# Token dispatch on one core: fp32 contraction replaced by three products of high and low parts, phi streamed per block, slot outputs kept in the slots' buffer

## The chip, the cores and the metric

The kernel runs on 1 core of one Trainium2 chip. The metric is the device time in microseconds (us) of one execution. TensorE (PE) multiplies matrices, VectorE (DVE), ScalarE (ACT) and GpSimd (POOL) work on elements, SyncE (SP) issues most DMAs. Each engine takes its instructions in order and waits on semaphores where the code says so.

## The reference

Two transformer layers with layer norms behind each half. The first three halves (dilated attention, a switch of 8 experts, linear attention) are hardly touched by the change. The last half is a soft mixture over 64 experts with 32 slots each:

```python
logits = jnp.einsum('bmd,dnp->bmnp', x, phi)
dispatch = jax.nn.softmax(logits, axis=0)
combine = jax.nn.softmax(logits.reshape(bsz, m, n * p), axis=-1).reshape(bsz, m, n, p)
slots = jnp.einsum('bmd,bmnp->bnpd', x, dispatch)
y = jnp.einsum('bnpd,nde->bnpe', slots, W) + b[None, :, None, :]
out = jnp.einsum('bnpd,bmnp->bmd', y, combine)
```

Here b is 4, m is 1024, d is 256, n*p is 2048. The dispatch softmax is taken over the 4 batch entries, so its sum (the "share" of each entry) is local to a token and a slot.

## The kernel before, in words

The program is a chain of stages, each a block in which every engine has its own instruction list: attention, routing, the 8 experts, linear attention (`linear_attention`), then `dispatch` and `combine`. Between stages all engines meet.

`dispatch` cuts the 2048 slots into 8 blocks of 256 columns (k) and the tokens into 8 chunks of 128 per batch entry (mc). A step (k, mc) handles all 4 batch entries. Blocks 1 to 7 are a hardware loop. In a step:

- TensorE computes the logits (`score`, L1621): 4 entries x 2 halves of d x 3 products of high and low parts (x high by phi high, x high by phi low, x low by phi high) in type fp32r, 24 matmuls of 256 columns. All of phi and its parts lie in SBUF; linear attention loads and splits them.
- ScalarE copies the logits from PSUM in two halves (L1688), and takes the exponential (L1706) behind VectorE's subtraction.
- VectorE takes the maximum over the 4 entries in three operations, each with one input in PSUM (L1778, L1780, L1782), subtracts it in two (L1786, L1788), inverts the sum of the step before (L1770), and reduces the rows to a maximum for the combine stage (L1793).
- GpSimd adds the four exponentials (L1730, L1732) and multiplies those of the step before by the inverse (`share`, L1723).
- TensorE contracts x with the shares three steps later (LAG is 3, `contract`, L1636): 8 matmuls in plain fp32, which run as 16 instructions.

Twice in a block, in steps 4 and 5, TensorE also runs an expert block (L1649): half of the y of the block before, 8 fp32 matmuls (16 instructions) into PSUM bank 1. VectorE adds the bias on the way to SBUF (`copy_y`, L1760, at the start of steps 5 and 6), and SyncE stores y. SyncE's list in a block is: the logits' store of each step (`keep`, L1575), behind those of steps 5 and 6 the four stores of one y half (L1568), and at the end the weights and the bias of all 8 experts of the block (L1562, L1563). The bias is there long before it is used.

Where PSUM is shared, a step's score waits for `less`, the count of VectorE's subtractions: in steps 5 and 6 for that of the step right before, in step 7 for both y halves to have left bank 1. In step 2 of a block ScalarE and VectorE each copy one half of the finished slots to SBUF.

## Time and profile before

| what | value |
|---|---|
| median of 3 runs | 1495.3 us (1493.47 to 1497.02) |
| the profiled execution | 1496.07 us, its span 1494.3 us |
| TensorE busy over the span | 92% |
| VectorE, ScalarE, GpSimd busy | 59%, 41%, 46% |
| granted TensorE clock, mean | 0.962 of 2.4 GHz |
| dispatch, then combine | 751 to 1245 us, 1245 us to the end |

The span runs from the first to the last instruction. A row of the timeline gives start and length in us, the engine, the line, the operation, output and inputs, and in brackets how long the engine was idle before and what released it. An engine's next instruction can start a little before the end of the one before is recorded, so what an instruction occupies is read from start to start.

### The profile page before, as it was taken

How to read it: one execution, taken by the hardware profiler on the slowest of the kernel's cores; microseconds unless marked ns; L12 is line 12 of the kernel's file. 1: busy time of each engine (PE TensorE's matmuls, PEld its weight loads, DVE VectorE, ACT ScalarE, POOL GpSimd, SP SyncE). 2: the span in 40 equal slices, each digit the busy share in tenths (PEclk: the TensorE clock that was granted, in tenths of full speed). 3: DMA queues.
4: the chain of work that ended last, by engine and by line, in shares of the span. 5: the costliest groups of instructions: out<-in, count | busy, mean ns of one | idle time of the engine just before them, and what ended most of it. 6: DMA issues, size and time to landing. Idle time of an engine off the chain costs nothing. (4 is left out here: it accounts for less than half of the span.)

```text
span 1494.3 us, 27884 instructions
## 1 busy us (share of the span) xinstructions
PE 1378.0 (92%) x8959; PEld 1203.4 (81%) x8960; DVE 877.4 (59%) x1763; ACT 612.8 (41%) x1077; POOL 683.3 (46%) x556
## 2 busy tenths in 40 slices
PE   7996599899999993899879999999999997999997
PEld 3454488788888883777669999999999977999997
DVE  5788422222222223577578787887887853666655
ACT  4554323233333331766543332332333324555553
POOL 6663287777660004340026665665655644350500
PEclk9998699999999996999979999999999998999999
DMA  4102325222310004310032264464463577465450
GB/s 166 60 28 94 119 81 149 95 98 101 124 70 14 14 15 134 120 57 1 1 127 85 85 183 123 142 170 110 146 193 96 157 222 270 154 214 184 147 201 31
DMA packets 109194, 171.17 MB, mean 115 GB/s; under 512 B 6128, under 2 KB 95088, under 8 KB 101712
## 3 DMA queue, kind: packets, MB, share of 16 engines
q1 hardware_dynamic: 100112, 156.00, 32.2%
q0 software_dynamic: 3408, 9.31, 2.2%
q10 hardware_dynamic: 5616, 5.11, 1.0%
q8 instruction: 33, 0.54, 0.2%
q14 instruction: 25, 0.20, 0.0%
HBM read 114.96 MB, written 55.44 MB: 114 GB/s over the span
## 5 line engine op out<-in xcount | busy, mean ns | idle before, releaser
L1636 PE MATMUL disp_psS<-disp_e,last_x 128*128 128x256 f32 x1024 | 233.1, 381 | 4.0 <-POOL disp_e L1723 4.0
L1636 PEld LDWEIGHTS disp_psS<-disp_e,last_x 128*128 128x128 f32 x1024 | 191.2, 191 | 28.6 <-POOL disp_e L1723 4.6
L1621 PE MATMUL disp_psL<-phi_hold,hand_xh 128*128 (+1 forms) x1024 | 199.8, 296 | 4.6 <-DVE disp_e L1788 4.4
L1730 POOL TENSOR_TENSOR disp_s<-disp_e 128x512 f32<-128x512 f32 x64 | 82.3, 1286 | 264.4 <-ACT disp_e L1706 264.4
L1909 PE MATMUL comb_psO<-phi_hold,comb_eh 128*128 (+1 forms) x1024 | 197.6, 290 | 0.4 <-DVE comb_el L2007 0.3
L1621 PEld LDWEIGHTS disp_psL<-phi_hold,hand_xh 128*128 128x128 f32 x1024 | 165.1, 193 | 8.5 <-issue 5.5
L1688 ACT ACTIVATE disp_raw<-disp_psL 128x512 f32<-128x512 f32 x128 | 76.4, 597 | 222.3 <-PE disp_psL L1621 157.8
L1909 PEld LDWEIGHTS comb_psO<-phi_hold,comb_eh 128*128 128x128 f32 x1024 | 156.3, 189 | 1.0 <-DVE comb_el L2007 0.9
L1723 POOL TENSOR_TENSOR disp_e<-disp_e,disp_rs 128x1024 f32<-128x1024 f32 x64 | 151.5, 2368 | 0.0
L1621 PE MATMUL disp_psL<-phi_hold 128*128 (+1 forms) x512 | 145.7, 285 | 0.0
L1909 PE MATMUL comb_psO<-phi_hold,comb_el 128*128 (+1 forms) x512 | 143.7, 281 | 0.0
L2007 DVE TENSOR_TENSOR comb_el<-comb_psT,comb_eh 128x512 fp32r<-128x512 f32 x128 | 88.1, 689 | 90.6 <-ACT comb_eh L1943 88.0
L972 PE MATMUL moe_psH<-w_hi,moe_xh 128*128 x312 | 129.1, 414 | 6.9 <-POOL w_lo L882 5.0
L1064 DVE TENSOR_TENSOR moe_hs<-moe_psH,moe_act_a 128x1024 f32<-128x1024 f32 x39 | 47.8, 1225 | 149.0 <-PE moe_psH L972 149.0
L972 PE MATMUL moe_psH<-w_lo,moe_xh 128*128 x312 | 125.6, 403 | 0.0
L972 PE MATMUL moe_psH<-w_hi,moe_xl 128*128 x312 | 125.6, 403 | 0.0
L1072 DVE TENSOR_TENSOR moe_hl<-moe_psHT,moe_hh 128x1024 fp32r<-128x1024 f32 x39 | 47.8, 1225 | 129.9 <-ACT moe_hh L1042 129.9
L1943 ACT ACTIVATE comb_eh<-comb_psT 128x512 fp32r<-128x512 f32 x128 | 76.3, 596 | 108.6 <-PE comb_psT L1895 108.5
L1770 DVE RECIPROCAL disp_rs<-disp_rs 128x256 f32<-128x256 f32 x64 | 111.5, 1743 | 0.5 <-POOL disp_rs L1732 0.5
L1166 POOL DMA_INDIRECT lin_yg<-sorted_y,table_place x32 | 32.1, 1002 | 172.3 <-POOLq L890 139.0
L1621 PEld LDWEIGHTS disp_psL<-phi_hold 128*128 128x128 f32 x512 | 98.8, 193 | 0.0
L1909 PEld LDWEIGHTS comb_psO<-phi_hold,comb_el 128*128 128x128 f32 x512 | 96.3, 188 | 0.0
(259 smaller groups left out, 3112.1 us busy)
## 6 DMA issues: line engine op xcount, KB each, us to landing
logits<-disp_raw SPq DMA_DIRECT2D x64, 512.0 KB, 4.1
hand_e<-logits SPq DMA_DIRECT2D x32, 1024.0 KB, 6.6
w_raw<-in_w SPq DMA_DIRECT2D x8, 2048.0 KB, 7.9
disp_wt<-in_w_slot SPq DMA_DIRECT2D x16, 1024.0 KB, 7.9
w_raw<-in_w SPq DMA_DIRECT2D x8, 1024.0 KB, 10.4
disp_bt<-in_b_slot SPq DMA_DIRECT2D x8, 1024.0 KB, 11.3
slot_y<-disp_yb SPq DMA_DIRECT2D x60, 128.0 KB, 3.2
comb_y_in<-slot_y SPq DMA_DIRECT2D x3, 2048.0 KB, 10.5
```

The lines of the kernel that those rows point to most:

```text
L972: last = nc.tensor.matmul(psH[:, n, :], xpart[:, k, :], wpart[:, bass.ds(b, 1), cols].rearrange("p a f -> p (a f)"), start=first, stop=k = ...
L1064: v.tensor_tensor(hs[:], psH[:, 2:4, :].rearrange("p a b -> p (a b)"), act_a[:], ALU.mult).then_inc(hs_ready, 1)
L1072: v.tensor_tensor(hl[:], psHT[:], hh[:].bitcast(F32), ALU.subtract).then_inc(hl_ready, 1)
L1621: last = nc.tensor.matmul(psL[p][:, b, :], xp[:, kd, t * P:(t + 1) * P], pp[:, kd, bass.ds(k * BLK, BLK)], start=b % 2 == 0 and kd == 0 an ...
L1636: last = nc.tensor.matmul(psS[kd][:, b, :], x[:, b * TB + mc, kd * P:(kd + 1) * P], e[mc % 4][:, b, :], start=mc == 0 and b % 2 == 0, stop ...
L1688: nc.scalar.activation(raw[mc % 4][:, half * 2:half * 2 + 2, :], psL[l_bank[mc]][:, half * 2:half * 2 + 2, :], ACT.Copy).then_inc(copied, 1)
L1723: nc.gpsimd.tensor_tensor(e[mc % 4][:], e[mc % 4][:], rs[mc % 2][:].unsqueeze(1).to_broadcast([P, B, BLK]), ALU.mult).then_inc(share_ready, 1)
L1730: nc.gpsimd.tensor_tensor(s2[:], e[mc % 4][:, 0:2, :], e[mc % 4][:, 2:4, :], ALU.add).then_inc(pair_sum, 1)
L1770: v.reciprocal(rs[mc % 2][:], rs[mc % 2][:]).then_inc(rsum_ready, 1)
L1909: last = nc.tensor.matmul(psO[j % 2][:, 0:D], ep[s % EB][:, i, :], yp[:, bass.ds(odd, 1), ch * D:(ch + 1) * D].rearrange("p a d -> p (a d) ...
L1943: nc.scalar.activation(eh[s % EB][:], psT[s % EB][:], ACT.Copy).then_inc(hi_ready, 1)
L2007: v.tensor_tensor(el[s % EB][:], psT[s % EB][:], eh[s % EB][:].bitcast(F32), ALU.subtract).then_inc(lo_ready, 1)
```

## The change: what it does

1. `contract` uses three fp32r products (x high by share high, x high by share low, x low by share high), 24 matmuls of 256 columns in place of 8 in fp32. The high part of the shares is a copy by ScalarE (`high_of_share`, 128x1024) two steps after the exponential (EH_LAG). The low part is a subtraction in place, entries 0 and 1 by VectorE (`first_rest`, 128x512, before the inversion), entries 2 and 3 by GpSimd (`second_rest`, 128x512, behind `share`).
2. The high part of x by rows (`natural`) is made by GpSimd in linear attention for 24 of 32 row tiles and by ScalarE in dispatch for 8; the low part by GpSimd at the start of dispatch, in 16 operations of 128x512 ahead of its first step, in the place of x.
3. The maximum over the entries takes two operations in place of three: one of 128x512 from PSUM into `pair`, one of 128x256 that reads both inputs from SBUF.
4. phi is loaded in blocks of 256 columns and split in dispatch (ScalarE and VectorE, 128x512 each, in step 4 of the block before). Linear attention no longer loads or splits it.
5. y is written over the half of the slots that its expert block has read, and stored from there. The bias has a buffer for 4 experts only: that of the second half is loaded behind the stores of the first.
6. Slots leave PSUM in two operations for each half of d, all four on ScalarE in the loop.
7. `combine` adds the low and the high part of x to the output, one more 128x256 operation of VectorE for each of 32 tiles. Some semaphores are merged, and the scratch for GpSimd's descriptors is 8192 bytes.

The core of the diff:

```diff
+            def load_bias(first):
+                sp.dma_start(bt[:], b_dram[bass.ds(first, HALF), :].partition_broadcast(P)).then_inc(b_loaded, 16)
...
-                        store(k - 1, last[y_step[mc - 1]], y_step[mc - 1], yb)
+                        h = y_step[mc - 1]
+                        store(k - 1, last[h], h)
+                        load_bias(last[1] if h == 0 else here)
...
-                wait(pe, share_ready, g + 1)
-                if isinstance(k, int) and k == 0 and mc == 0:
-                    wait(pe, lo, PIECES)
+                wait(pe, first_low, g + 1)
...
-                        last = nc.tensor.matmul(psS[kd][:, b, :], x[:, b * TB + mc, kd * P:(kd + 1) * P], e[mc % 4][:, b, :],
-                                                start=mc == 0 and b % 2 == 0, stop=mc == MC - 1, skip_group_check=True)
+                        if kd == 0 and b == 2:
+                            wait(pe, second_low, g + 1)
+                        row, cols = b * TB + mc, slice(kd * P, (kd + 1) * P)
+                        for a, (xp, ep) in enumerate(((natural, eh[mc % 2]), (natural, el[mc % 4]), (natural_lo, eh[mc % 2]))):
+                            last = nc.tensor.matmul(psS[kd][:, b, :], xp[:, row, cols], ep[:, b, :],
+                                                    start=mc == 0 and b % 2 == 0 and a == 0, stop=mc == MC - 1 and a == 2,
+                                                    skip_group_check=True)
                 last.then_inc(gone, 1)
...
+            def high_of_share(g, mc):
+                wait(act, share_ready, g + 1)
+                wait(act, gone, g - 1)
+                nc.scalar.activation(eh[mc % 2][:], e[mc % 4], ACT.Copy).then_inc(eh_ready, 1)
...
+                wait(act, kept[mc % 4], k * (MC // 4 * 16) + mc // 4 * 16)
+                wait(act, peaked, g - 3)
+                copy_half(g, mc, 1)
+                wait(act, top_ready, 2 * g + 1)
+                copy_half(g, mc, 0)
+                if mc >= EH_LAG or not fresh:
+                    high_of_share(g - EH_LAG, (mc - EH_LAG) % MC)
+                if mc == SPLIT_AT:
+                    high_of_phi(k + 1, after)
                 if mc == EVAC and not fresh:
                     wait(act, gone, k * MC)
...
+                    evacuate(0)
+                wait(act, less, 2 * g + 2)
+                nc.scalar.activation(e[mc % 4], e[mc % 4], ACT.Exp).then_inc(exp_ready, 1)
+                if mc == EVAC and not fresh:
+                    evacuate(1)
...
+            def natural_rest(n):
+                wait(pool, turned, n + 1)
+                wait(pool, hi, highs(n) + n % 2)
+                nc.gpsimd.tensor_tensor(rows_of(natural_lo, n), rows_of(x, n), rows_of(natural, n).bitcast(F32),
+                                        ALU.subtract).then_inc(natural_low, 1)
+
+            def second_rest(g, mc):
+                wait(pool, eh_ready, g + 1)
+                nc.gpsimd.tensor_tensor(el[mc % 4][:, 2:4, :], e[mc % 4][:, 2:4, :], eh[mc % 2][:, 2:4, :].bitcast(F32),
+                                        ALU.subtract).then_inc(second_low, 1)
...
-
+                    second_rest(g - 1, (mc - 1) % MC)
+
+            for n in range(PIECES):
+                natural_rest(n)
...
+            def first_rest(g, mc):
+                wait(dve, eh_ready, g + 1)
+                v.tensor_tensor(el[mc % 4][:, 0:2, :], e[mc % 4][:, 0:2, :], eh[mc % 2][:, 0:2, :].bitcast(F32),
+                                ALU.subtract).then_inc(first_low, 1)
...
+            def copy_y(k, h, bank=Y_BANK):
                 wait(dve, y_raw, k * 2 + (h + 1))
-                wait(dve, b_loaded, k * 16 + 16)
-                wait(dve, stored, k * (2 * 16 * B) + h * (16 * B))
-                v.tensor_tensor(yb[:], psL[Y_BANK][:], bt[:, h * HALF:(h + 1) * HALF, :],
-                                ALU.add).then_inc(y_ready, 1)
+                wait(dve, b_loaded, k * 32 + (h + 1) * 16)
...
-                v.tensor_tensor(t[:], psl[:, 0, :], raw[mc % 4][:, 2, :], ALU.max).then_inc(top_ready, 1)
-                wait(dve, top_ready, 3 * g + 1)
-                v.tensor_tensor(t[:], psl[:, 1, :], t[:], ALU.max).then_inc(top_ready, 1)
-                wait(dve, top_ready, 3 * g + 2)
-                v.tensor_tensor(t[:], psl[:, 3, :], t[:], ALU.max).then_inc(top_ready, 1)
+                v.tensor_tensor(pair[:], psl[:, 0:2, :], raw[mc % 4][:, 2:4, :], ALU.max).then_inc(top_ready, 1)
+                wait(dve, top_ready, 2 * g + 1)
+                v.tensor_tensor(t[:], pair[:, 0, :], pair[:, 1, :], ALU.max).then_inc(top_ready, 1)
                 wait(dve, gone, g - 3)
-                wait(dve, top_ready, 3 * g + 3)
+                wait(dve, top_ready, 2 * g + 2)
                 both = t[:].unsqueeze(1).to_broadcast([P, 2, BLK])
                 v.tensor_tensor(e[mc % 4][:, 2:4, :], psl[:, 2:4, :], both, ALU.subtract).then_inc(less, 1)
                 wait(dve, copied, 2 * g + 2)
                 v.tensor_tensor(e[mc % 4][:, 0:2, :], psl[:, 0:2, :], both, ALU.subtract).then_inc(less, 1)
+                if mc >= EH_LAG or not fresh:
+                    first_rest(g - EH_LAG, (mc - EH_LAG) % MC)
                 if mc > 0 or not fresh:
                     invert(g - 1, (mc - 1) % MC)
-                if mc == EVAC and not fresh:
-                    copy_slots(k)
+                if mc == SPLIT_AT:
+                    low_of_phi(k + 1, after)
                 v.tensor_reduce(rowmax[:].rearrange("p (b j) k -> p b j k", b=B)[:, :, mc, bass.ds(k, 1)].rearrange("p b a -> p (b a)"),
                                 raw[mc % 4][:], X, ALU.max).then_inc(peaked, 1)
 
             for mc in range(MC):
-                step(0, mc, fresh=True)
...
-                v.scalar_tensor_tensor(xo[:, j, :], psO[j % 2][:, 0:D], rden[:, j % 2:j % 2 + 1], row(t), ALU.mult, ALU.add).then_inc(summed, 1)
-                wait(dve, summed, t + 1)
+                v.scalar_tensor_tensor(xo[:, j, :], psO[j % 2][:, 0:D], rden[:, j % 2:j % 2 + 1],
+                                       natural_lo[:, bass.ds(t, 1), :].rearrange("p a d -> p (a d)").bitcast(F32), ALU.mult, ALU.add).then_inc(summed, 1)
+                wait(dve, summed, 2 * t + 1)
+                v.tensor_tensor(xo[:, j, :], xo[:, j, :], natural[:, bass.ds(t, 1), :].rearrange("p a d -> p (a d)").bitcast(F32),
+                                ALU.add).then_inc(summed, 1)
+                wait(dve, summed, 2 * t + 2)
```

Three places where the order of instructions moves. First GpSimd, the looped part of dispatch, two steps of before (`disp_s` is the pairwise sum, `disp_rs` the sum and its inverse, `disp_e` the exponentials and shares):

```order
L1730 TENSOR_TENSOR disp_s<-disp_e 128x512 [waits disp_sum_ready,disp_exp_ready]
L1732 TENSOR_TENSOR disp_rs<-disp_s 128x256 [waits disp_pair_sum]
L1723 TENSOR_TENSOR disp_e<-disp_e,disp_rs 128x1024 [waits disp_rsum_ready]
L34 REGISTER_ALU
L1730 TENSOR_TENSOR disp_s<-disp_e 128x512 [waits disp_sum_ready,disp_exp_ready]
L1732 TENSOR_TENSOR disp_rs<-disp_s 128x256 [waits disp_pair_sum]
L1723 TENSOR_TENSOR disp_e<-disp_e,disp_rs 128x1024 [waits disp_rsum_ready]
```

The same place now (`disp_eh`, `disp_el` are the high and low parts of the shares; 7965 to 7968 are the four buffers of `disp_e`):

```order
L1803 TENSOR_TENSOR disp_s<-disp_e_7965 128x512 [waits disp_sum_ready,disp_exp_ready]
L1805 TENSOR_TENSOR disp_rs<-disp_s 128x256 [waits disp_pair_sum]
L1796 TENSOR_TENSOR disp_e_7968<-disp_e_7968,disp_rs 128x1024 [waits disp_rsum_ready]
L1791 TENSOR_TENSOR disp_el<-disp_e_7968,disp_eh 128x512 [waits disp_eh_ready]
L34 REGISTER_ALU
L1803 TENSOR_TENSOR disp_s<-disp_e_7966 128x512 [waits disp_sum_ready,disp_exp_ready]
L1805 TENSOR_TENSOR disp_rs<-disp_s 128x256 [waits disp_pair_sum]
L1796 TENSOR_TENSOR disp_e_7965<-disp_e_7965,disp_rs 128x1024 [waits disp_rsum_ready]
L1791 TENSOR_TENSOR disp_el<-disp_e_7965,disp_eh 128x512 [waits disp_eh_ready]
```

Each step has gained L1791, which waits for ScalarE's high part, ahead of the next step's sum. Second, ScalarE in one step of the loop now (before, the two copies of the logits L1688 and the exponential L1706 alone):

```order
L1735 ACTIVATE disp_raw<-disp_psL 128x512 [waits disp_peaked,disp_kept2,disp_logits]
L34 ISA
L1735 ACTIVATE disp_raw<-disp_psL 128x512 [waits disp_top_ready]
L1728 ACTIVATE disp_eh<-disp_e_7965 128x1024 [waits disp_gone,disp_share_ready]
L34 REGISTER_ALU
L1760 ACTIVATE disp_e_7967<-disp_e_7967 128x1024 [waits disp_less]
```

The high part of a share (L1728) stands ahead of the exponential of two steps later (L1760). Third, VectorE around the second y copy of the loop, now:

```order
L1868 TENSOR_TENSOR disp_top<-disp_pair 128x256 [waits disp_top_ready]
L34 REGISTER_ALU [waits disp_gone]
L1872 TENSOR_TENSOR disp_e_7966<-disp_psL,disp_top 128x512 [waits disp_top_ready]
L1874 TENSOR_TENSOR disp_e_7966<-disp_psL,disp_top 128x512 [waits disp_copied]
L1836 TENSOR_TENSOR disp_el<-disp_e_7968,disp_eh 128x512 [waits disp_eh_ready]
L1858 RECIPROCAL disp_rs<-disp_rs 128x256 [waits disp_sum_ready]
L1881 ISA
L1881 TENSOR_REDUCE last_rowmax<-disp_raw 128x4
L34 REGISTER_ALU
L34 REGISTER_ALU [waits disp_y_raw]
L1846 TENSOR_TENSOR disp_slots<-disp_psL,disp_bt 128x1024 [waits disp_b_loaded]
L34 ISA
```

L1868 and L1836 read both inputs from SBUF and are new. The y copy, L1846, waits for the bias, and all of step 6 on VectorE is queued behind it.

## Rows read from the trace of the kernel before

**Rows 1.** Busy time in one stretch of the dispatch, by engine (columns as named).

```profile
880.00:930.00 50.00, 50.00 (x308) 46.38 (x308) 39.66 (x50) 16.31 (x22) 29.29 (x22) 1.00 0.42 115
```

**Rows 2.** Timeline of TensorE: start, length, idle before in brackets.

```profile
862.78 0.28 PE L1621 MATMUL disp_psL<-phi_hold 128*128 x1
...
863.14 0.28 PE L1621 MATMUL disp_psL<-phi_hold 128*128 x1
...
865.42 3.62 PE L1636 MATMUL disp_psS<-disp_e,last_x 128*128 128x256 f32 x16
868.69 0.59 PE L1621 MATMUL disp_psL<-phi_hold,hand_xh 128*128 x2
```

**Rows 3.** Timeline of the same step: VectorE, ScalarE and GpSimd.

```profile
866.25 0.42 DVE L1778 TENSOR_TENSOR disp_top<-disp_psL,disp_raw 128x256 f32<-128x256 f32 x1 [0.93 <-ACT disp_raw L1688]
866.71 0.42 DVE L1780 TENSOR_TENSOR disp_top<-disp_psL,disp_top 128x256 f32<-128x256 f32 x1
...
867.62 0.69 DVE L1786 TENSOR_TENSOR disp_e<-disp_psL,disp_top 128x512 f32<-128x512 f32 x1
...
868.83 1.74 DVE L1770 RECIPROCAL disp_rs<-disp_rs 128x256 f32<-128x256 f32 x1
868.95 1.06 ACT L1706 ACTIVATE disp_e<-disp_e 128x1024 f32<-128x1024 f32 x1 [1.19 <-DVE disp_e L1788]
...
870.08 1.29 POOL L1730 TENSOR_TENSOR disp_s<-disp_e 128x512 f32<-128x512 f32 x1 [1.92 <-ACT disp_e L1706]
...
870.49 1.16 DVE L1793 TENSOR_REDUCE last_rowmax<-disp_raw 128x1024 f32 x1
...
871.46 0.73 POOL L1732 TENSOR_TENSOR disp_rs<-disp_s 128x256 f32<-128x256 f32 x1
...
872.14 2.36 POOL L1723 TENSOR_TENSOR disp_e<-disp_e,disp_rs 128x1024 f32<-128x1024 f32 x1
```

**Rows 4.** Timeline of the two steps with an expert block, third block of slots.

```profile
900.54 3.62 PE L1649 MATMUL disp_psL<-disp_wt,disp_slots 128*128 128x256 f32 x16
...
908.62 0.60 ACT L1688 ACTIVATE disp_raw<-disp_psL 128x512 f32<-128x512 f32 x1 [0.95 <-DVE disp_top L1780]
...
910.05 2.48 SPq L1568 DMA_DIRECT2D slot_y<-disp_yb  x4
...
914.55 1.22 DVE L1760 TENSOR_TENSOR disp_yb<-disp_psL,disp_bt 128x1024 f32<-128x1024 f32 x1 [1.45 <-DMA slot_y<-disp_yb]
...
917.49 0.42 DVE L1778 TENSOR_TENSOR disp_top<-disp_psL,disp_raw 128x256 f32<-128x256 f32 x1 [1.71 <-ACT disp_raw L1688]
```

**Rows 5.** Groups by line: count, then least, median and largest ns.

```profile
L1498 POOL TENSOR_TENSOR phi_hold<-hand_y,phi_hold x4: 1258/2336/2356, 1236.0 to 1242.9; 128x1024 fp32r<-128x1024 f32 x3, 128x512 fp32r<-128x512 f32 x1
L1498 DVE TENSOR_TENSOR phi_hold<-hand_y,phi_hold x1: 684/684/684, 1251.7 to 1251.7; 128x512 fp32r<-128x512 f32 x1
...
L1491 ACT ACTIVATE phi_hold<-hand_y x5: 612/1038/1056, 1234.8 to 1250.9; 128x1024 fp32r<-128x1024 f32 x3, 128x512 fp32r<-128x512 f32 x2
```

**Rows 6.** Timeline of the last stage: VectorE and GpSimd side by side.

```profile
1281.58 0.73 POOL L1884 TENSOR_TENSOR phi_hold<-comb_y_in,phi_hold 128x256 fp32r<-128x256 f32 x1
...
1281.76 0.57 DVE L47 TENSOR_TENSOR comb_mean<-comb_stats 128x4 f32<-128x4 f32 x1
...
1282.26 0.15 DVE L48 TENSOR_TENSOR comb_var<-comb_stats 128x4 f32<-128x4 f32 x1
```

**Rows 7.** Timeline, start of the dispatch: its first contraction.

```profile
780.09 1.13 PE L1636 MATMUL disp_psS<-disp_e,last_x 128*128 128x256 f32 x4 [1.97 <-POOL disp_e L1723]
```

**Rows 8.** Timeline of TensorE: last looped expert block, and the final pair.

```profile
1188.41 1.89 PE L1649 MATMUL disp_psL<-disp_wt,disp_slots 128*128 128x256 f32 x8
...
1228.64 7.14 PE L1649 MATMUL disp_psL<-disp_wt,disp_slots 128*128 128x256 f32 x32 [1.52 <-DVE disp_slots L1765]
```

**Rows 9.** DMA issues of the page: count, KB each, median us to landing.

```profile
logits<-disp_raw SPq DMA_DIRECT2D x64, 512.0 KB, 4.1
...
disp_bt<-in_b_slot SPq DMA_DIRECT2D x8, 1024.0 KB, 11.3
```

More of the change, by code:

```diff
@@ L1180, in _ @@
                     fetch(t)
[L1181 to L1182 removed]
+            pool.wait_ge(constants_set, KB + 2)
+            for t in range((B - 1) * TB):
+                natural_high(t)
         @block.tensor
@@ new lines, in step @@
+            def step(k, mc, after, fresh=False):
+                g = k * MC + mc
+                wait(act, logits, g + 1)
+                wait(act, kept[mc % 4], k * (MC // 4 * 16) + mc // 4 * 16)
[7 more added lines that the diff above has]
+                    high_of_phi(k + 1, after)
@@ L1711, in _ @@
                 for mc in range(MC):
-                    step(k, mc)
-            step(NBLK, EVAC, draining=True)
+                    step(k, mc, bass.ds(other, 1))
+            for mc in range(MC - EH_LAG, MC):
+                high_of_share((NBLK - 1) * MC + mc, mc)
+            wait(act, gone, NBLK * MC)
+            evacuate(0)
             act.wait_ge(hand.neg_ready, 2)
```

244 lines of the change are left out of this document (138 added, 106 removed).

## The prediction, made before the changed kernel ran

> **What bounds the kernel now.** I read the busy shares first, then a stretch inside the dispatch, then a step of it engine by engine. In the stretch TensorE is busy 50.00 of 50.00 us at full clock, VectorE 39.7, GpSimd 29.3, ScalarE 16.3 [rows 1]. So today nothing but TensorE's own work sets the dispatch, and a cheaper contraction would be gained in full, as long as the other three stay hidden. Two numbers for that. A triple of fp32r products takes 863.14 - 862.78 = 0.36 us, 0.12 per matmul; a contraction takes 868.69 - 865.42 = 3.27, and the fp32r matmul behind it starts about 0.18 late (the first row's length is 0.59, not about 0.40), so 3.45 in all [rows 2]. A step is then 24 x 0.12 + 3.45 = 6.33.
>
> The other engines, start to start [rows 3]: on GpSimd pair sum to sum 1.38, sum to share 0.68, share 2.36, so 4.42 from the first to the end. On VectorE a 256-column maximum 0.46, the two subtractions 1.21 (one 0.61, its length 0.69), the inversion 1.66, the row maximum about 1.09. On ScalarE the exponential 1.06. GpSimd was idle 1.92 before its pair sum and VectorE 0.93 before its maximum: this is the whole cover, a step.
>
> A block of 8 steps and two expert blocks takes (1188.41 - 900.54) / 5 = 57.57 us [rows 4, 8]. In its sixth step the second y copy waits 1.45 for the store of the first half, and still VectorE is idle 1.71 before its next maximum: harmless today [rows 4].
>
> **The change, part by part.**
>
> TensorE: a contraction falls from 3.45 to 24 x 0.12 = 2.88. That is 0.57 a step; 64 of them are 36 us. That gain exists only if a step of the others fits in 5.76.
>
> The loop through GpSimd and ScalarE. The new low part on GpSimd waits for ScalarE's high part, which waits for the share, and the next pair sum stands behind it. So a step cannot be shorter than: pair sum to share end 4.42 [rows 3], high part of 1024 columns 1.04, low part of 512 columns on GpSimd 1.26 [rows 5], three hand-overs of about 0.04 to 0.08 (exponential end 870.01, pair sum 870.08): **6.85 us**. This loop did not exist before. It is above 5.76 and also above 6.33.
>
> The second SBUF input. VectorE's new 256-column maximum and its low part read two operands from SBUF; the old ones had one in PSUM. The trace of the last stage shows what such an operation does beside GpSimd: an operation on 4 columns starts at 1281.76, takes 0.57 and ends at 1282.33, just behind the GpSimd operation that ends at 1282.31, and the next one like it takes 0.15 [rows 6]. So it waits until the running GpSimd operation is over. In the new step the maximum comes when the share is under way: VectorE's low part ends, inversion 1.66, row maximum 1.09, the 512-column maximum with its hand-over 0.73, together 3.48 after the pair sum started, while the share runs from 2.06 to 4.42. The chain of a step becomes: share end 4.42, maximum 0.46, first subtraction 0.61, second 0.69, exponential 1.06, hand-overs 0.15: 7.39. Then VectorE's low part, held until GpSimd's own low part ends (4.42 + 0.04 + 1.04 + 0.08 + 1.26 = 6.84), has read for 0.66 more, to **7.5 us** a step, which I take. The bounds are 6.85 (no such wait) and 7.5.
>
> The Trainium skill states this as a rule ("SBUF — State Buffer", Who interferes with whom): a VectorE instruction with two SBUF inputs contends with a GpSimd instruction that reads SBUF, and whichever starts first holds the shared port for its whole length. The trace agrees. By the rule a step is 7.5, without it 6.85.
>
> The bias. The load for the second half is issued only behind the four stores of the first half. The logits' copy of step 5 ends, and 0.83 later the first store is issued (909.22 to 910.05), which take 2.48 [rows 4]; then the load. Its landing is bounded by a store of the same 512 KB, 4.1, and half of the 1024 KB bias load, 5.65 [rows 9]. Counted from the pair sum of step 3 in a block (0): share, maximum and exponential of step 4 put its sum at 7.5; phi's low part, held behind the sum, and the row maximum bring VectorE to 11.25; first y copy to 12.4 (1.15 [rows 4]); logits' copy of step 5 over at 13.7; stores to 17.05; load issued at 17.25, landed at 21.35 to 22.9. TensorE's second expert block is done at about 15.9 and step 6's logits could be used at 19.85, so VectorE now stands still for the bias, and the maximum of step 6 comes at 22.55 to 24.1. The pair sum of step 6 follows 4.3 later (0.73 + 0.60 + 1.04 + 0.66 + 1.26), at 26.9 to 28.4. Five more steps of 7.5 and 0.3 for ScalarE's copy of the slots ahead of an exponential: a block is 64.7 to 66.2, middle 65.4, **+7.8** over 57.57. Queued behind the y copy is all of VectorE's step 6, and TensorE's step 7, which needs bank 1, waits too. Had the load landed in time, step 6's sum would be at 24.15 and a block at 62.0.
>
> Start of the dispatch. It begins at about 751 with a load of phi, 3 us by my estimate (under the 4.1 of 512 KB [rows 9]), ahead of ScalarE's first high part, then GpSimd does its 16 subtractions, 16 x 1.22 = 19.5, from about 755.2 to 774.7. Two sums, a share, high and low part add 4.1 + 2.4 + 1.1 + 0.7, to 783.0, and the exponential of step 1, itself about 2 later, to at most 785; I take 784.8 in place of 780.09 [rows 7]. Nine steps of 7.5, 0.3 for the slots, 0.6 for phi's low part and 2.9 for a contraction bring the first expert block to 856.1, where it was 900.54 - 57.57 = 842.97: **+13.1**. Six blocks of 7.8: **+46.8**.
>
> The end. From the last looped expert block to the final pair was 1228.64 - 1188.41 = 40.2 [rows 8]. Now 27.65 to the pair sum of step 6, 7.5 to that of step 7, then two shares with their high and low parts and the last contraction, 14.6, and 1.7 to the expert block as before, less the 3.0 by which it starts behind the sum: 48.45, **+8.2**. The last y half waits for a bias load too: four stores and 4.1 to 5.65 of landing against no wait, less a quicker last store: 1 to 5, I take **+3**. Combine: one more operation of VectorE a tile, of which the last shows, **+0.5**.
>
> At nothing: linear attention loses two copies of phi on ScalarE and 16 subtractions on GpSimd and gains 24 operations there, beside a TensorE that they did not hold up; the merged semaphores keep their order; the smaller scratch could hold GpSimd's gathers back by up to a landing of 4.1 [rows 9]; they come ahead of stages that no row shows short of them, and I take 0.
>
> Sum: 13.1 + 46.8 + 8.2 + 3 + 0.5 = 71.6 on the profiled execution's 1496.07, 0.8 above the median of the runs, so about **1566**.
>
> **The rivals.**
>
> No wait for the second SBUF input. The 0.57 was seen on tiny operations; if large ones interleave, a step is 6.85. Then the first expert block comes 7.3 later, a block takes 60.3 (+2.7, six of them 16.4), the end costs 4.9 + 3 + 0.5: +32, about 1528. With the bias in time too, a block is 57.4 and the total about 1507. Rows 6 speak against it.
>
> TensorE stays the bound, the other side. If GpSimd's and ScalarE's loop were shorter than 5.76 (it decides at 5.76; my sum says 6.85), a block would be 57.57 - 8 x 0.57 = 53.0, less 36 in all, plus 4.7 at the start and 3 at the end: 1467. For it: 50.00 of 50.00 us busy, and spacings of new pairs of operations that no row shows. Against it: 1.1 us a step would have to vanish from instructions whose lengths are in the rows.
>
> A lower TensorE clock. TensorE would now idle 7.5 - 5.76 = 1.7 a step, and longer at the bias. The clock was lower behind the gap at the start: contraction instructions there start 1.13 / 4 = 0.28 apart, not 0.20 [rows 2, 7]. At half clock a step of TensorE is 11.5; six such steps among 64 add 24: about 1590.
>
> **How the numbers follow.** The forecast, loop, second input and bias together, 0.57; no wait for the second input 0.16, and with the bias in time 0.04; TensorE the bound 0.11; the clock case or worse 0.12. The first two hold 0.73. The range from 1520 to 1588 takes in the step between 6.85 and 7.5, the bias between 4.1 and 5.65, and part of the clock case, some 0.8. A change of under 0.2% (3 us) could not be told from none; faster 0.12, same 0.03, slower 0.85.
>
> **What would show it.** In the looped part: pair sums on GpSimd 7.5 us apart (6.85 in the first rival, 5.8 in the second), ended by ScalarE; the 256-column maximum recorded at well over 0.46, ending with the share; VectorE's second y copy waiting some 3 to 4 us for the bias; blocks of 65 us; TensorE busy about 80% of the dispatch; gaps of TensorE put down to the low parts of VectorE or GpSimd. I am wrong if TensorE is still without gaps there. The weakest step is the maximum that meets the share: a VectorE that comes 1.4 us earlier or later in the cycle misses it.

## The result, and the profile after the change

| kernel | median | runs |
|---|---|---|
| before | 1494.38 us | 1492.98 to 1497.02, 4 runs |
| changed | 1562.43 us | 1560.84 to 1562.88, 4 runs |

The ratio is 1.0447, 95% interval 1.0434 to 1.0460: the change makes the kernel 68 us slower. The forecast was 1566, range 1520 to 1588.

From the page of the changed kernel: span and busy times.

```profile
span 1559.1 us, 29192 instructions
...
PE 1363.3 (87%) x9471; PEld 1201.8 (77%) x9472; DVE 1011.9 (65%) x1799; ACT 683.7 (44%) x1178; POOL 807.4 (52%) x644
```

TensorE's share falls from 92% to 87%, VectorE's rises from 59% to 65% and GpSimd's from 46% to 52%. Busy times of the stretch that [rows 1] showed (PE, PEld, DVE, ACT, POOL; then granted clock, DMA share, GB/s):

```profile
880.00:930.00 50.00, 42.07 (x329) 40.44 (x330) 49.52 (x49) 24.16 (x32) 38.20 (x28) 1.00 0.51 142
```

TensorE, 50.00 of 50.00 before, is down to 42.07 (84%; about 80 was forecast). VectorE has gone from 39.66 to 49.52: in this stretch it has no gap left. One step of the loop, VectorE, then GpSimd, then ScalarE, against [rows 3]:

```profile
956.17 1.16 DVE L1881 TENSOR_REDUCE last_rowmax<-disp_raw 128x1024 f32 x1
957.25 0.67 DVE L1866 TENSOR_TENSOR disp_pair<-disp_psL,disp_raw 128x512 f32<-128x512 f32 x1
957.95 1.24 DVE L1868 TENSOR_TENSOR disp_top<-disp_pair 128x256 f32<-128x256 f32 x1
959.23 0.69 DVE L1872 TENSOR_TENSOR disp_e<-disp_psL,disp_top 128x512 f32<-128x512 f32 x1
959.84 0.68 DVE L1874 TENSOR_TENSOR disp_e<-disp_psL,disp_top 128x512 f32<-128x512 f32 x1
960.43 1.48 DVE L1836 TENSOR_TENSOR disp_el<-disp_e,disp_eh 128x512 fp32r<-128x512 f32 x1
961.83 1.74 DVE L1858 RECIPROCAL disp_rs<-disp_rs 128x256 f32<-128x256 f32 x1
...
956.50 2.41 POOL L1796 TENSOR_TENSOR disp_e<-disp_e,disp_rs 128x1024 f32<-128x1024 f32 x1
960.08 1.28 POOL L1791 TENSOR_TENSOR disp_el<-disp_e,disp_eh 128x512 fp32r<-128x512 f32 x1 [1.17 <-ACT disp_eh L1728]
961.68 1.37 POOL L1803 TENSOR_TENSOR disp_s<-disp_e 128x512 f32<-128x512 f32 x1 [0.32 <-ACT disp_e L1760]
963.13 0.74 POOL L1805 TENSOR_TENSOR disp_rs<-disp_s 128x256 f32<-128x256 f32 x1
...
958.94 1.06 ACT L1728 ACTIVATE disp_eh<-disp_e 128x1024 fp32r<-128x1024 f32 x1 [0.40 <-POOL disp_e L1796]
960.55 1.06 ACT L1760 ACTIVATE disp_e<-disp_e 128x1024 f32<-128x1024 f32 x1 [0.54 <-DVE disp_e L1874]
```

Read it as a circle. GpSimd's share (L1796) starts at 956.50 and ends at 958.91. VectorE's 256-column maximum (L1868), which reads both inputs from SBUF, starts at 957.95 and takes 1.24, where the shortest of its 64 in this trace takes 0.42: it ends at 959.19, 0.28 behind the share. Then subtractions, exponential (960.55), and the pair sum (L1803) at 961.68, which waited for ScalarE. It started at 954.36 the step before: 7.32. VectorE's low part (L1836) starts 0.35 behind GpSimd's own (L1791) and takes 1.48, ending 0.55 behind it. Who waited for whom between 780 and 1300 us (total us, times, longest):

```profile
PE disp_psS L1668 <- DVE disp_el L1836: 66.4, 46, 4.3
...
DVE disp_slots L1846 <- DMA disp_bt<-in_b_slot: 18.3, 7, 3.0
```

TensorE, which had no gap in the stretch of [rows 1], now waits 66.4 us for VectorE's low part. Its contraction did get cheap, 0.11 to 0.12 us from one fp32r product to the next once it runs:

```profile
961.97 0.38 PE L1668 MATMUL disp_psS<-disp_eh,last_natural 128*128 128x256 f32 x1 [1.37 <-DVE disp_el L1836]
962.19 0.28 PE L1668 MATMUL disp_psS<-disp_el,last_natural 128*128 128x256 f32 x1
```

The second half's bias, third block of slots: the y copies on VectorE, and SyncE's four stores and load.

```profile
931.48 1.21 DVE L1846 TENSOR_TENSOR disp_slots<-disp_psL,disp_bt 128x1024 f32<-128x1024 f32 x1
...
941.96 1.23 DVE L1846 TENSOR_TENSOR disp_slots<-disp_psL,disp_bt 128x1024 f32<-128x1024 f32 x1 [2.46 <-DMA disp_bt<-in_b_slot]
...
934.75 2.46 SPq L1579 DMA_DIRECT2D slot_y<-disp_slots  x4
937.41 0.38 SPq L1574 DMA_DIRECT2D disp_bt<-in_b_slot  x1
```

The load is issued at 937.41, behind the stores, and the copy waits 2.46 us for it. Expert blocks: the first of the third block, the last looped one, and the final pair.

```profile
923.59 3.62 PE L1682 MATMUL disp_psL<-disp_wt,disp_slots 128*128 128x256 f32 x16
...
1241.37 3.62 PE L1682 MATMUL disp_psL<-disp_wt,disp_slots 128*128 128x256 f32 x16
...
1290.58 7.14 PE L1682 MATMUL disp_psL<-disp_wt,disp_slots 128*128 128x256 f32 x32 [1.65 <-DVE disp_slots L1852]
```

A block takes (1241.37 - 923.59) / 5 = 63.56 us; it was 57.57 [rows 4, 8].

### The profile page after: what moved, and what is told of

The parts are those of the page before. It is cut to its first block and busy times, and to the rows that moved or that the text cites. A ratio compares the mean times of both kernels' runs of the same rounds, so it can differ in the third digit from the quotient of the medians.

```text
span 1559.1 us, 29192 instructions
## 1 busy us (share of the span) xinstructions
PE 1363.3 (87%) x9471; PEld 1201.8 (77%) x9472; DVE 1011.9 (65%) x1799; ACT 683.7 (44%) x1178; POOL 807.4 (52%) x644
## 5 line engine op out<-in xcount | busy, mean ns | idle before, releaser
L1668 PE MATMUL disp_psS<-disp_eh,last_natural 128*128 128x256 f32 x512 | 151.0, 295 | 66.8 <-DVE disp_el L1836 66.4
L2000 PE MATMUL comb_psO<-hand_parts,comb_eh 128*128 (+1 forms) x1024 | 198.6, 292 | 1.7 <-DVE comb_el L2102 1.7
L1649 PE MATMUL disp_psL<-disp_ph,hand_xh 128*128 (+1 forms) x512 | 150.4, 294 | 18.1 <-DVE disp_slots L1846 9.3
L2000 PEld LDWEIGHTS comb_psO<-hand_parts,comb_eh 128*128 128x128 f32 x1024 | 156.9, 190 | 2.8 <-issue 1.8
L1668 PEld LDWEIGHTS disp_psS<-disp_eh,last_natural 128*128 128x128 f32 x512 | 98.8, 193 | 76.7 <-DVE disp_el L1836 76.4
L1796 POOL TENSOR_TENSOR disp_e<-disp_e,disp_rs 128x1024 f32<-128x1024 f32 x64 | 157.2, 2456 | 0.0
L1649 PE MATMUL disp_psL<-disp_pl,hand_xh 128*128 (+1 forms) x512 | 146.7, 287 | 0.0
L1649 PE MATMUL disp_psL<-disp_ph,hand_xl 128*128 (+1 forms) x512 | 146.4, 286 | 0.0
L1668 PE MATMUL disp_psS<-disp_el,last_natural 128*128 128x256 f32 x512 | 145.6, 284 | 0.0
L1668 PE MATMUL disp_psS<-disp_eh,last_natural_lo 128*128 128x256 f32 x512 | 145.4, 284 | 0.0
L2000 PE MATMUL comb_psO<-hand_parts,comb_el 128*128 (+1 forms) x512 | 144.0, 281 | 0.0
L1791 POOL TENSOR_TENSOR disp_el<-disp_e,disp_eh 128x512 fp32r<-128x512 f32 x64 | 82.7, 1292 | 106.2 <-ACT disp_eh L1728 106.2
L1649 PEld LDWEIGHTS disp_psL<-disp_ph,hand_xh 128*128 128x128 f32 x512 | 100.1, 195 | 20.2 <-issue 19.9
```

The costliest lines, as they stand in the source:

```text
L1649: last = nc.tensor.matmul(psL[p][:, b, :], xp[:, kd, t * P:(t + 1) * P], pp[:, half, kd, :].rearrange("p a n -> p (a n)"), start=b % 2 == ...
L1668: last = nc.tensor.matmul(psS[kd][:, b, :], xp[:, row, cols], ep[:, b, :], start=mc == 0 and b % 2 == 0 and a == 0, stop=mc == MC - 1 and ...
L1791: nc.gpsimd.tensor_tensor(el[mc % 4][:, 2:4, :], e[mc % 4][:, 2:4, :], eh[mc % 2][:, 2:4, :].bitcast(F32), ALU.subtract).then_inc(second_l ...
L1796: nc.gpsimd.tensor_tensor(e[mc % 4], e[mc % 4], rs[mc % 2][:].unsqueeze(1).to_broadcast([P, B, BLK]), ALU.mult).then_inc(share_ready, 1)
L2000: last = nc.tensor.matmul(psO[j % 2][:, 0:D], ep[s % EB][:, i, :], yp[:, bass.ds(odd, 1), ch * D:(ch + 1) * D].rearrange("p a d -> p (a d) ...
```

## Experiments

All were compared with the kernel before on their own chip, so their ratios can be set against 1.0447. Blocks are the distance between two expert blocks.

**Is TensorE still the bound?** One fp32 product of the high parts in place of three; the low parts are computed and waited for, but left out of the product.

```diff
-for a, (xp, ep) in enumerate(((natural, eh[mc % 2]), (natural, el[mc % 4]), (natural_lo, eh[mc % 2]))):
-    last = nc.tensor.matmul(psS[kd][:, b, :], xp[:, row, cols], ep[:, b, :], ...
+last = nc.tensor.matmul(psS[kd][:, b, :], natural[:, row, cols].bitcast(F32), eh[mc % 2][:, b, :].bitcast(F32), ...
```

> The contraction is one plain fp32 product of the high parts (8 matmuls, 3.45 us as before the change) in place of three fp32r products (2.88); the low parts of shares and x are still computed and waited for, but left out of the product. My theory: TensorE is no longer the bound in the dispatch, its step of 6.33 is hidden under 7.32, so the time stays within 3 us of 1562.4, perhaps 1 to 2 more from the first and last contractions; pair sums still 7.3 apart. Rival: TensorE's own work still counts in full, +0.57 x 64 = +36, 1599.

Measured: 1559.83, ratio 1.0415 (1.0391 to 1.0440); +36 would be 1.069. Busy times of the stretch from 880 to 930 us:

```profile
880.00:930.00 50.00, 45.75 (x280) 41.63 (x279) 49.52 (x49) 24.27 (x32) 38.33 (x28) 1.00 0.50 142
```

TensorE is busy 3.7 us more and the time does not rise. Plain steps are even 0.05 shorter (7.27 for 7.32); why is not shown. The change's gain of 0.57 a step is worth nothing here, and its loss comes from the other engines.

**The two meetings, one at a time.** First without VectorE's low part (entries 0 and 1 in two products), the maximum as changed:

```diff
-                if mc >= EH_LAG or not fresh:
-                    first_rest(g - EH_LAG, (mc - EH_LAG) % MC)
```

> The changed kernel without VectorE's low part of the shares (entries 0 and 1 are contracted in two products, their low part is left out); the maximum still reads both inputs from SBUF. My theory, after the first runs: there are two meetings of VectorE and GpSimd, and each alone makes a loop: the maximum held until the share is over (7.3), and the low parts, where whichever engine starts first holds the other (7.4). Here the first is left: pair sums 7.2 to 7.3 apart, maximum 1.2 and longer, VectorE with gaps; 64 x 0.1 less, 1550 to 1562. Rival: the step was 7.32 because VectorE's list was full; 1.40 taken from it lets the loop through the high part set the step, 6.85, 1532.

Measured: 1547.79, ratio 1.0347 (1.0321 to 1.0374), a gain of 15; plain steps of 7.2.

```profile
954.13 2.55 DVE L1870 TENSOR_TENSOR disp_top<-disp_pair 128x256 f32<-128x256 f32 x1
...
954.00 2.40 POOL L1798 TENSOR_TENSOR disp_e<-disp_e,disp_rs 128x1024 f32<-128x1024 f32 x1
```

The maximum is now 2.55 us long. VectorE, with 1.4 us less to do, reaches it earlier and is only held longer, until the share is over. The rival (a full VectorE sets the step) would have given 6.85 and falls. The total is 2 us below the range forecast: the step that splits phi went from 8.54 to 7.64, which I had not counted, while the wait for the bias grew to 3.8 to 4.5 us a block (2.3 to 3.0 in the changed kernel).

Then the maximum as before, from PSUM, and VectorE's low part kept:

```diff
-v.tensor_tensor(pair[:], psl[:, 0:2, :], raw[mc % 4][:, 2:4, :], ALU.max).then_inc(top_ready, 1)
-wait(dve, top_ready, 2 * g + 1)
-v.tensor_tensor(t[:], pair[:, 0, :], pair[:, 1, :], ALU.max).then_inc(top_ready, 1)
+v.tensor_tensor(t[:], psl[:, 0, :], raw[mc % 4][:, 2, :], ALU.max).then_inc(top_ready, 1)
+wait(dve, top_ready, 3 * g + 1)
+v.tensor_tensor(t[:], psl[:, 1, :], t[:], ALU.max).then_inc(top_ready, 1)
+wait(dve, top_ready, 3 * g + 2)
+v.tensor_tensor(t[:], psl[:, 3, :], t[:], ALU.max).then_inc(top_ready, 1)
```

> The maximum over the entries is put back to three 128x256 operations with one input in PSUM; all else as in the changed kernel. My theory: the maximum that is held until the share is over sits in the loop that sets the step (pair sum to share start 2.15, share 2.41, held maximum 0.32, subtractions 1.31, exponential 1.13: 7.32). Without it the loop through the high part and GpSimd's low part is left, 6.85: pair sums 6.8 to 7.0 apart, no VectorE maximum over 0.5, VectorE with gaps again, 64 x 0.47 = 30 less, 1532 us. Rival: VectorE is simply full (it has no gap in the changed kernel) and the operations take what they take; three of 0.46 are 0.22 more than 0.70 and 0.46, so a step grows and the time goes to 1576. Second rival: the hold moves on to the low part, step 7.1, 1548.

Measured: 1558.04, ratio 1.0405 (1.0387 to 1.0422), a gain of 4 by the medians and 6 by the ratios, where I expected 30.

```profile
961.59 0.69 DVE L1836 TENSOR_TENSOR disp_el<-disp_e,disp_eh 128x512 fp32r<-128x512 f32 x1 [1.41 <-ACT disp_eh L1728]
...
955.99 1.28 POOL L1803 TENSOR_TENSOR disp_s<-disp_e 128x512 f32<-128x512 f32 x1
...
961.63 1.79 POOL L1791 TENSOR_TENSOR disp_el<-disp_e,disp_eh 128x512 fp32r<-128x512 f32 x1 [1.17 <-ACT disp_eh L1728]
963.38 1.28 POOL L1803 TENSOR_TENSOR disp_s<-disp_e 128x512 f32<-128x512 f32 x1
```

My first theory falls here in part. The maximum is 0.42 again, but VectorE is now early, and its low part (961.59) starts 0.04 before GpSimd's (961.63). Now GpSimd is held: 1.79 in place of 1.28. The pair sum behind it comes 7.39 after the last one: the loop of 6.85 and the hold of about 0.5. My second rival had this mechanism, with 7.1 for its size. The Trainium skill says so ("SBUF — State Buffer", Who interferes with whom): the order of issue decides who blocks. The traces agree, with 1.48 for VectorE behind GpSimd above, and 1.79 for GpSimd behind VectorE here.

Then both taken away, by the two edits together:

> Both meetings taken away: maximum in three operations with an input in PSUM, and VectorE's low part left out (entries 0 and 1 in two products). My theory: the loop pair sum, sum, share, high part, GpSimd's low part is left: 1.35 + 0.69 + 2.38 + 1.13 + 1.30 = 6.85, pair sums 6.8 to 6.9 apart, ended by GpSimd's own low part; 64 x 0.47 = 30 less than the changed kernel, 1532. The wait for the bias is as before or up to 1 longer a block. Rival: GpSimd's operations are slowed by VectorE's reads in general, also with one SBUF input; then the step stays over 7.1 and the time over 1548.

Measured: 1523.88, ratio 1.0189 (1.0165 to 1.0213), 39 less than the changed kernel.

```profile
951.16 1.28 POOL L1793 TENSOR_TENSOR disp_el<-disp_e,disp_eh 128x512 fp32r<-128x512 f32 x1 [1.17 <-ACT disp_eh L1730]
952.40 1.29 POOL L1805 TENSOR_TENSOR disp_s<-disp_e 128x512 f32<-128x512 f32 x1
953.77 0.74 POOL L1807 TENSOR_TENSOR disp_rs<-disp_s 128x256 f32<-128x256 f32 x1
954.47 2.40 POOL L1798 TENSOR_TENSOR disp_e<-disp_e,disp_rs 128x1024 f32<-128x1024 f32 x1
958.04 1.27 POOL L1793 TENSOR_TENSOR disp_el<-disp_e,disp_eh 128x512 fp32r<-128x512 f32 x1 [1.17 <-ACT disp_eh L1730]
```

Pair sum to pair sum in plain steps is 6.85 to 6.88: high part, low part, pair sum, sum and share in a row, the loop of the forecast. Blocks fall from 63.6 to 59.2, more than eight steps of 0.47, since the step that splits phi falls from 8.5 to 7.1. Of the 40.3 us between the two spans 26.3 are in the six blocks and 7.0 at the start, where the first expert block came 98.8 us after the dispatch's first transpose, not 105.8. The wait for the bias grew to 4.1 to 4.3 us a block, by more than the 1 I had allowed.

**The new maximum alone, in the kernel before.**

> The kernel before, with only the maximum of the change (one 128x512 operation from PSUM, one 128x256 that reads both inputs from SBUF). My theory: the new maximum is held behind the share here too, recorded at 1.2 to 1.5 us against 0.42, but TensorE is the bound at 6.33 a step, and GpSimd, which waited 1.92 before each pair sum, still waits about 1.1: no change, 1495 +- 3. Rival: the hold reaches TensorE through the logits' banks in the steps with an expert block, +1 a step there, +16 in all.

Measured: 1517.09, ratio 1.0141 (1.0124 to 1.0158): 21 us slower, although nothing of TensorE's 6.33 a step had changed. The loss is under 2%, but its interval is clear of 1.

```profile
948.17 2.49 DVE L1781 TENSOR_TENSOR disp_top<-disp_pair 128x256 f32<-128x256 f32 x1
950.69 0.69 DVE L1785 TENSOR_TENSOR disp_e<-disp_psL,disp_top 128x512 f32<-128x512 f32 x1
...
948.01 2.37 POOL L1724 TENSOR_TENSOR disp_e<-disp_e,disp_rs 128x1024 f32<-128x1024 f32 x1
953.14 1.27 POOL L1731 TENSOR_TENSOR disp_s<-disp_e 128x512 f32<-128x512 f32 x1 [2.77 <-ACT disp_e L1707]
...
960.34 1.26 POOL L1731 TENSOR_TENSOR disp_s<-disp_e 128x512 f32<-128x512 f32 x1 [2.78 <-ACT disp_e L1707]
```

My theory was wrong. The maximum, 0.42 alone, takes 2.49, and the pair sums stand 7.20 apart. The idle times of 0.93 and 1.92 [rows 3] were no cover, since each step's delay is the next step's starting point: the share ends, 0.28 later the maximum, subtractions to the exponential at 1.63, pair sum 1.13 later, share 2.04 behind that, and it runs 2.38. That circle is 7.18, longer than 6.33, and seven of a block's eight steps take it (the eighth, with the expert blocks in it, 8.9): 59.2 a block against 57.57.

**The bias.** SyncE issues the load ahead of the stores:

```diff
-                        store(k - 1, last[h], h)
+                        wait(sp, y_ready, (k - 1) * 2 + (h + 1))
                         load_bias(last[1] if h == 0 else here)
+                        store(k - 1, last[h], h)
```

> SyncE issues the load of the next half's bias ahead of the four stores of y, not behind them; nothing else differs. My theory: the second y copy of a block waits 2.46 us for a load that is issued 2.66 later than it could be, and all of VectorE's sixth step is queued behind it; seven waits of 2.46 go and part of the last one of 6.05 (1.8): 1562.4 - 17.2 - 1.8 = 1543.5, blocks of 61.2. Rival: the wait is covered, since TensorE's second expert block and the loop through GpSimd would be late anyway; then the wait is put down to another releaser and the time falls by less than 8. Second rival: the load lands later when it competes with the logits' store, a wait of 1 stays, 1553.

Measured: 1550.48, ratio 1.0362 (1.0345 to 1.0379), 13 less where 19 were expected.

```profile
937.59 1.20 DVE L1847 TENSOR_TENSOR disp_slots<-disp_psL,disp_bt 128x1024 f32<-128x1024 f32 x1
...
1061.93 1.22 DVE L1847 TENSOR_TENSOR disp_slots<-disp_psL,disp_bt 128x1024 f32<-128x1024 f32 x1 [2.07 <-DMA disp_bt<-in_b_slot]
...
932.94 0.37 SPq L1574 DMA_DIRECT2D disp_bt<-in_b_slot  x1
```

In the third block (first row) the wait is gone, and the block takes 61.2, as forecast; in the fifth (second row) it is 2.07, and each later block has one of 1.6 to 2.3. But the stores now run beside the load, whose median landing rises from 4.6 to 5.7 us, and 5 of the 16 copies still wait, 12.2 us together, against 8 and 24.3: the second rival, in part. The mean block is 62.1.

**Other orders.** Maximum from PSUM and bias first, and: the exponential ahead of the high part, GpSimd's low part behind the next pair sum, VectorE's behind the row maximum.

> Nothing left out. Maximum from PSUM, bias load first, and three orders changed so that no engine waits for the high part: ScalarE takes the exponential ahead of the high part, GpSimd's low part of two steps before stands between pair sum and sum, VectorE's low part behind the row maximum. My theory: the loop of 6.85 is gone, GpSimd's own work is 5.7 and TensorE's 5.76; the way from a score over copies, maximum, exponential, pair sum and low part to the contraction (6.9 and 5.76 for two steps) gives 6.4; VectorE's low part meets a busy GpSimd and adds up to 0.6: step 6.4 to 6.9, 1500 to 1530, most likely 1510. Rival: GpSimd has no gap any more, VectorE's low part is held behind the share of 2.4 in each step and the loop closes through it: step over 7.2, 1540 or more.

Measured: 1549.13, ratio 1.0353 (1.0328 to 1.0378). Plain steps are 6.8 to 6.9 (one of a block 6.2) as expected, but the step that copies the slots takes 8.4 and the two with an expert block 10.2 and 9.1 to 10.9. The total is the rival's, its step of over 7.2 is not. Beside the edits named, four of its blocks still wait for the bias, up to 2.9 us.

```profile
958.21 1.60 DVE L1839 TENSOR_TENSOR disp_el<-disp_e,disp_eh 128x512 fp32r<-128x512 f32 x1
...
957.97 1.28 POOL L1792 TENSOR_TENSOR disp_el<-disp_e,disp_eh 128x512 fp32r<-128x512 f32 x1
959.21 1.19 POOL L1808 TENSOR_TENSOR disp_rs<-disp_s 128x256 f32<-128x256 f32 x1
```

VectorE's low part is held behind GpSimd's to 1.60, then GpSimd's sum behind it to 1.19 (0.73 alone). The hold is passed on, not hidden. What the long steps cost each is not separated.

The whole low part on VectorE, the orders left alone (maximum from PSUM and bias first here too):

```diff
-v.tensor_tensor(el[mc % 4][:, 0:2, :], e[mc % 4][:, 0:2, :], eh[mc % 2][:, 0:2, :].bitcast(F32), ...
+v.tensor_tensor(el[mc % 4][:], e[mc % 4][:], eh[mc % 2][:].bitcast(F32), ...
-                    second_rest(g - 1, (mc - 1) % MC)
```

> Nothing left out, all 8 entries' products as in the changed kernel. Maximum from PSUM, bias load first, and the whole low part (128x1024) made by VectorE, none by GpSimd; orders as in the changed kernel. My theory: the loop then runs share end, high part 1.08, exponential 1.0, pair sum, sum, share: 4.45 + 0.04 + 1.04 + 1.0 + 0.05 = 6.6, VectorE's own list is 6.55, its low part of 1.2 falls into the time in which GpSimd waits for the exponential, so nobody is held: step 6.6 to 6.8, 1500 to 1512. Rival: the low part starts late enough to meet the pair sum, one holds the other for up to 1.2 as in the run with the maximum from PSUM alone; step 7.2 or more, 1535 and up.

Measured: 1517.67, ratio 1.0154 (1.0135 to 1.0172).

```profile
953.85 1.22 DVE L1833 TENSOR_TENSOR disp_el<-disp_e,disp_eh 128x1024 fp32r<-128x1024 f32 x1
...
954.88 1.34 POOL L1802 TENSOR_TENSOR disp_s<-disp_e 128x512 f32<-128x512 f32 x1 [2.16 <-ACT disp_e L1759]
```

128x1024 in 1.22 us while GpSimd waits, steps of 6.6 to 6.7 in the plain ones. It is the best version with three products for all entries, 44 us below the changed kernel with nothing left out. The total is 6 over the range. The step that copies the slots takes 7.6, with two of ScalarE's copies ahead of the exponential (960.39 and 960.87, the exponential at 961.35), and the two around the split of phi take 7.2 and 7.9, on a VectorE without a gap there. How much of the 44 us is the moved low part is not isolated: no run has the other two edits alone together; one at a time they gave 6 and 13.

**The added operation of combine**, left out (one run):

> The changed kernel without its added operation in combine (the high part of x is left out of the output). The transposes of combine stretch over 1545.4 - 1306.9 = 238.5 us in the changed kernel and 1481.1 - 1245.3 = 235.8 before, 2.7 more, where only 0.5 was forecast. My theory: the added 128x256 operation reads both inputs from SBUF and is held by GpSimd, which makes high and low parts of y for half of the stage; without it the stretch is 235.8 to 236.3. Rival: the 2.7 come from the start of the stage (lower clock, later y), and it stays at 238.

The transposes of combine stretch from 1305.9 to 1542.3, 236.4 us, against 238.5 with the operation and 235.8 before: about 2.1 of the 2.7 are its own, just over the range of my theory, and the rival's 238 falls. It is one run; the seven other versions with the changed combine gave 237.7 to 238.6. The run took 1557.26. The traces say where it comes from: in the changed kernel only 7 of the 32 added operations are held, to 0.60 to 0.95 against 0.42, each ending 0.28 behind one of GpSimd's, and in this stage TensorE waits for VectorE three times, 1.7 us together; before it was 0.3, and without the operation there is no such wait.

**A version from the findings.** Entries 0 and 1 in plain fp32, 2 and 3 in three products. VectorE copies half of the slots again, and combine has its added operation for half of the tiles only. Core of the edit:

```diff
+wait(pe, share_ready, g + 1)
+    for b in range(2):
+        last = nc.tensor.matmul(psS[kd][:, b, :], x[:, b * TB + mc, kd * P:(kd + 1) * P], e[mc % 4][:, b, :], ...
+wait(pe, second_low, g + 1)
+    for b in range(2, B):
+        for a, (xp, ep) in enumerate(((natural, eh[mc % 2]), (natural, el[mc % 4]), (natural_lo, eh[mc % 2]))):
```

> Nothing left out. Entries 0 and 1 are contracted in plain fp32 as before the change, entries 2 and 3 in three fp32r products, so that VectorE has no low part of shares, ScalarE's high part is 128x512, and GpSimd makes the one low part of 128x512; maximum from PSUM, bias load first, exponential ahead of the high part, low part between pair sum and sum. TensorE's step is 2.88 + 1.64 + 0.18 + 1.44 = 6.14 against 6.33 before the change. My theory: no operation of VectorE in a step reads two inputs from SBUF, so nothing is held, GpSimd's 5.75 hides, TensorE is the bound again: 64 x 0.19 = 12 less than the kernel before, 5 to 8 more for phi's load and the low parts at the start of the dispatch: 1490, range 1484 to 1498. Rival: GpSimd at 5.75 of 6.14 is late for the contraction, step 6.4 to 6.6, 1505 to 1515.

Measured: 1496.34, ratio 1.0009 (0.9992 to 1.0026), inside the range and 6 over its middle. Busy times of a stretch, and first and last looped expert block and the last y copy:

```profile
900.00:950.00 50.00, 49.89 (x347) 47.14 (x346) 42.45 (x56) 21.39 (x32) 39.76 (x29) 1.00 0.59 163
```

```profile
845.88 3.62 PE L1686 MATMUL disp_psL<-disp_wt,disp_slots 128*128 128x256 f32 x16
...
1180.58 3.62 PE L1686 MATMUL disp_psL<-disp_wt,disp_slots 128*128 128x256 f32 x16
...
1235.06 1.22 DVE L1850 TENSOR_TENSOR disp_slots<-disp_psL,disp_bt 128x1024 f32<-128x1024 f32 x1 [7.91 <-DMA disp_bt<-in_b_slot]
```

TensorE is the bound again (49.89 of 50.00), and a block takes (1180.58 - 845.88) / 6 = 55.78, 1.8 below the kernel before. Of these 10.7 us in the profiled execution the rest takes back 2.0 from the dispatch's first transpose to its first expert block, 1.4 in the last steps, 1.5 before combine, where the last y copy waits 7.91 for its bias, 2.1 in combine, and it began 1.0 later. Two more edits went for the stretch before combine.

> The half split, with one edit more: the bias of the very last y half is loaded into a logits buffer that is free by then, ahead of the last expert blocks, instead of behind the y copy of the first half. Nothing left out. My theory: in the half split VectorE's last y copy waited 7.91 us for this load, and the first matmul of combine came 18.2 behind the last expert pair, against 16.6 in the kernel before; without the wait the last copy follows the second half of the pair after about 2, so 5.5 go: 1490.8, ratio to the kernel before 0.996 to 0.998, the first kernel here below it. Rival: combine's start waits for the stores and loads of y and logits and not for that copy; then nothing changes, ratio 1.001.

> The half split with the early last bias, and the four low parts of the first y (one input each of three 128x1024 and one 128x512) made by VectorE at the end of the dispatch and not by GpSimd. Nothing left out. My theory: with the bias in time, the dispatch ended with GpSimd's four low parts (8.18 us from 1232.42 to 1240.60, combine's first matmul at 1241.8); VectorE needs about 4.1 for them from 1234.5 on and ends at 1238.6, so 2 go: ratio 0.998, about 1492. Rival: stores, loads and the meeting of all engines hold the start of combine; no change, 0.999.

Measured: 1494.10, ratio 0.999 (0.998 to 1.000), and 1494.59, ratio 0.9995 (0.9983 to 1.0006). Final pair to combine falls from 18.2 to 15.7 and 15.2 us: 2.5 and 0.5, where 5.5 and 2 were expected. The totals moved by about what the measurement can tell: these versions undo the loss, and a gain over the kernel before is not shown.

## Why the prediction was right

The sum was made on the profiled execution: +71.6 forecast (which gives 1567 by its own rule, not 1566), and 1559.1 - 1494.3 = +64.8 measured between the spans. The mechanism is right. That the total is so near is in part luck: 10.8 too much in the blocks and 3.4 at the last bias stand against 3.1, 0.8, 0.8 and 2.7 too little elsewhere. By its own terms:

- **Contraction 2.88, and TensorE no longer the bound**: right; a contraction takes 2.92 from its start to the next product (median). 42.07 of 50.00 us busy, and a dearer contraction changes nothing.
- **The loop of 6.85**: right, shown with nothing else in the way (6.85 to 6.88).
- **The second SBUF input**: the mechanism is right, shown by both single removals. The chain through the maximum was forecast at 7.39 and is 7.32. The last addition, that VectorE's held low part carries the step on to 7.5, failed: the inversion behind it ends at 963.57, while the share waits for GpSimd's own sum until 963.83. What I did not see is that taking away one of the two meetings brings so little: 6 and 15 us, both together 39.
- **The bias**: from the pair sum of step 3 to that of step 6, 946.74 - 920.40 = 26.3, forecast 26.9 to 28.4; the load was issued 17.0 behind the first (forecast 17.25), and the wait was 2.3 to 3.0, not 3 to 4. Six blocks: +36.0 for +46.8. Of the miss about 7 is this stretch (26.4 on the mean against 27.65) and about 4 the other five steps (37.15 against 37.8). It is the largest miss.
- **Start of the dispatch, +13.1**: from its first transpose (754.16) to its first expert block (859.97) it is 105.8, against 842.97 - 751.10 = 91.9: +13.9, right, with two misses that cancel: 35.9 to the first contraction, where 33.7 was forecast, and 69.9 from there, for 71.3. The stretch also varies: with the bias issued first, the same code up to there, it was 108.4 (see the last section). But it began 3.1 later, where I took 0. Of this 1.9 is in linear attention: from its first transpose to that of the dispatch 157.2 to 158.0 us in the twelve profiles with the changed code, and 155.6 and 155.8 in the two with the old. It is also 157.2 to 157.6 in the three with 8 of the 24 new GpSimd operations, so their number is not the cause; which edit is, stays open. The other 1.1 lie inside the scatter of the stages before (594.4 to 598.2 at linear attention's first transpose).
- **The end, +8.2**: 1290.58 - 1241.37 = 49.2, against 40.2: +9.0, right.
- **The last bias, +3**: wrong, -0.4 (16.3 us from the final pair to combine, 16.6 before). The y copy does wait 6.05 for the load, but the 16.6 held a wait of another kind, which I had not seen. Combine starts when the last store of y has landed. In the kernel before the last four stores landed 6.5 us after their issue (median), beside the loads of the logits, and in the changed kernel, issued later, after 2.3. That the wait for the bias costs something is shown by the load issued first (16.3 to 14.5, a wait of 4.29) and by the half split (18.2 to 15.7).
- **Combine, +0.5**: +3.2. The tail behind the last matmul is 0.5 longer, as forecast; 2.7 are in the stretch before, which I had counted as covered by TensorE, and 2.1 of them go with the operation.
- **The clock**: 1.00 in each stretch of 50 us from 850 to 1200, with gaps of 1.4 us; the rival of a lower clock didn't come. With less work for TensorE (the first of the two-product runs) it was 0.94 to 0.97 in the four stretches from 850 to 1050. The 0.28 between contraction instructions that the rival took from [rows 7] is the length of a merged row through four; their starts are at 780.09, 780.40, 780.62 and 780.84, and the granted clock from 779 to 783 was 0.79, so the clock was lower there, but by less than the rival says.

## What to carry to other kernels

In these traces a VectorE operation that reads both inputs from SBUF is priced by what GpSimd is doing when it comes, not by its length, and if its result leads back to GpSimd's next operation, the meeting closes a circle that slack does not open: sum the circle and compare it with the bound. Keep one input in PSUM, or give the work to VectorE whole and into a gap of GpSimd, rather than half to each. Where several such circles have nearly the same length (here 7.2, 7.3 and 7.4), removing one shows little (6 and 15 us of 39); remove all in one kernel before you judge any.
